# Expert blocks in two phases, the first of them ahead of the last tiles' routing, with downward products in fp16

## The chip, the cores and the metric

One core of one Trainium2 chip runs the kernel. The metric is device time in microseconds of one execution. Three runs of the kernel before gave 682.38, 676.74 and 687.29 us, median 682.38.

## What is computed

Two layers on x of 32 sequences with 128 tokens of 256 values (T = 32 tiles of 128 tokens). Each layer is an attention and a feed-forward part, each added to x. The change is in the first layer. Its feed-forward part is a mixture of E = 8 experts with hidden size H = 512, of which each token takes two:

```python
def _L0_xattn_ref(Q, K):                       # Q = layernorm(x), K = ctx
    scores = jnp.einsum('btd,bsd->bts', K, K)
    scores = scores * jnp.tril(jnp.ones((Lq, Lq)))[None, :, :]
    return Q + jnp.einsum('bts,bsd->btd', scores, Q)

def _L0_ffn_ref(x, w12, w3, gate_w):           # x = layernorm(x)
    scores = jnp.einsum('btd,ed->bte', x, gate_w)
    topk_scores, topk_idx = jax.lax.top_k(scores, TOP_K)      # TOP_K = 2
    topk_probs = jax.nn.softmax(topk_scores, axis=-1)
    ...
    h12 = jnp.einsum('btd,ehd->bteh', x, w12)
    h1, h2 = (h12[..., :H], h12[..., H:])
    hidden = jax.nn.silu(h1) * h2
    expert_out = jnp.einsum('bteh,edh->bted', hidden, w3)
    return jnp.sum(total_probs[..., None] * expert_out, axis=-2)
```

## The kernel before

There is one instruction stream for each engine; engines wait for each other by semaphores written out by hand, so the order in the code is the order on the engine.

**The attention** (`sync0`, `pool0`, `act0`, `pe0`, `dve0`) goes over 32 tiles in steps s. TensorE makes the scores (L588), the gate products (L598) and the product with y (L609, writes x1 together with VectorE's L666). VectorE masks scores (L662) and takes moments. In the same steps a tile's normed row z is made and split into a high and a low fp16 part (`make_z`, `high_z` on ScalarE, `low_z` L774 on VectorE), and six groups of tiles (`ROUTES`) are routed: `choose` picks the two experts of each token, TensorE's `rank` counts, `put_down` gives each row its place in its expert's region. POOL then scatters each tile's rows twice (L504, once for each choice) into `z_rows` in DRAM, which is sorted by expert. ScalarE takes the squares of w12 (L530) for its scale. The tables `z_step`, `w12_step`, `w3_step` and `square_at` say at which step each load or part stands. SyncE (SP) loads context, x and weights in its queue.

**Between** attention and blocks the last tiles are routed and scattered. For the first PRE = 3 experts ScalarE and VectorE split w12 in high and low fp16 parts (L538, L782) and w3 in two fp32r parts (L540, L785). `block_tables` finds for each of NB = 71 blocks of 128 rows its first row, its expert and its scale.

**The expert blocks** (`sync1`, `pool1`, `act1`, `pe1`, `dve1`), j = 0 to 70, sorted by expert. SP's `load(j)` turns 128 rows of z by DMA (four buffers), `load_told` fetches each row's token number and gap, eight blocks at a time. VectorE's `hold` (L1176) copies the block's expert w12 into one of two buffers. TensorE's `up` is 48 products of 128 columns (L1084), ScalarE takes the silu (L1136), VectorE the hidden row (L1184, `hidden`), ScalarE its high part (L1143), VectorE its low part (L1190, `rest_g`), and TensorE's `down` is 12 products of 256 columns (L1097). `keep_y` (L1152) weighs the result. TensorE's order is up(j + 1), down(j). Before a block eight `weigh` operations (L1197 on) turn told rows into weights. POOL splits the weights of experts 3 to 7 (`prepare`, L1038 to L1043), and then hands the blocks' rows out to their tokens by an adding DMA (`hand_out`, L1053). A block of expert e waits in `hold` until `w_ready` counts e + 1.

**The second layer** follows (222 us) and is the same in both kernels.

## Time and profile of the kernel before

The profiled execution took 683.7 us; the median of the runs is 682.4.

| engine | busy us | share of the span | instructions |
|---|---|---|---|
| TensorE (PE) | 559.4 | 82% | 5902 |
| weight loads (PEld) | 487.4 | 71% | 5902 |
| VectorE (DVE) | 509.4 | 75% | 1475 |
| ScalarE (ACT) | 359.4 | 53% | 662 |
| GpSimd (POOL) | 391.1 | 57% | 469 |

The DMA engines moved 87.2 MB. In 40 slices of 17.1 us each, in tenths of busy time, TensorE stands at

```profile
PE   5887772055989999999999999990777676899997
DVE  5997867666698877666666565642999688999997
POOL 1064554779999998888884434332002023888655
PEclk9765665568999999999999999996799999999999
```

The first row has a hole at slices 7 and 8 (120 to 137 us) and one at 27 (462 to 479). PEclk is the granted TensorE clock in tenths of full speed. An average over the span mixes stretches with different limits, so the rows below are taken by stretch.

### The profile page before, as it was taken

To read this page: it belongs to the slowest core of one execution; us is meant where nothing else is said; L and a number is where in the kernel's file an instruction comes from. 1 tells how busy PE (TensorE), PEld (TensorE's weight loads), DVE (VectorE), ACT (ScalarE), POOL (GpSimd) and SP (SyncE) were. 2 spreads that over 40 slices of the span, in tenths; PEclk is the share of its full clock that TensorE was granted. 3 is DMA by queue.
4 is the path that set the end of the run, shared out by engine and by line. 5 is a ranking of instruction groups with operands and counts; after the bars stand their busy time and mean duration, and the time that the engine had idled before them with its cause. 6 is when DMAs were issued, how large, how long until landed. Compare 5 with 4: busy or idle time off the path is not lost.

```text
span 683.7 us, 17743 instructions
## 1 busy us (share of the span) xinstructions
PE 559.4 (82%) x5902; PEld 487.4 (71%) x5902; DVE 509.4 (75%) x1475; ACT 359.4 (53%) x662; POOL 391.1 (57%) x469
## 2 busy tenths in 40 slices
PE   5887772055989999999999999990777676899997
PEld 5776661035989999999999999990655453566765
DVE  5997867666698877666666565642999688999997
ACT  2254647622334444434444444430667957999995
POOL 1064554779999998888884434332002023888655
PEclk9765665568999999999999999996799999999999
DMA  8598993436444514787986654447795300011112
GB/s 308 185 310 295 360 363 132 149 78 156 86 127 88 133 26 61 91 101 90 104 98 78 67 64 65 72 86 199 232 356 168 102 17 1 10 47 40 40 39 79
DMA packets 103166, 87.23 MB, mean 128 GB/s; under 512 B 55075, under 2 KB 94883, under 8 KB 102054
## 3 DMA queue, kind: packets, MB, share of 16 engines
q1 hardware_dynamic: 89782, 68.27, 35.7%
q0 software_dynamic: 13296, 17.83, 16.2%
q8 instruction: 50, 0.82, 0.5%
q14 instruction: 38, 0.31, 0.2%
HBM read 44.35 MB, written 32.41 MB: 112 GB/s over the span
## 4 chain that ended last, share of the span: by engine, by line
PE 58%; DVE 19%; issue 8%; ACT 5%; DMA 2%; SPq 2%; DVEq 0%; ACTq 0%; another core or an unknown queue 0%; POOLq 0%
PE banks L1084 25%; PE banks L1097 14%; PE banks L1726 4%; PE banks L1702 3%; PE banks L1705 2%; PE banks L1716 2%; PE banks L598 1%; ACT work L555 1%; PE banks L609 1%; DVE w_parts L782 1%; DVE h_rounded L1990 1%; DVE ffn_amax L1963 1%; ACT hidden_ffn L1595 1%; DVE x_rows L1754 1%; DVE hidden_T_low L1190 1%
## 5 line engine op out<-in xcount | busy, mean ns | idle before, releaser
L1084 PE MATMUL banks<-z_turned,w_of_block 128*128 128x128 f16 x3408 | 203.9, 220 | 0.7 <-DMA z_turned<-z_rows 0.3
L1084 PEld LDWEIGHTS banks<-z_turned,w_of_block 128*128 128x128 f16 x3408 | 192.0, 98 | 4.4 <-issue 1.5
L1053 POOL DMA_INDIRECT rows_of_tokens<-x_rows,row_tokens x71 | 121.4, 1710 | 77.9 <-ACT x_rows L1152 50.6
L1184 DVE SCALAR_TENSOR_TENSOR hidden_T<-banks,blk_inv,silu_T 128x512 f32<-128x512 f32 x71 | 53.3, 751 | 87.7 <-PE banks L1084 87.3
L1143 ACT ACTIVATE hidden_T_high<-hidden_T 128x512 fp32r<-128x512 f32 x71 | 44.9, 632 | 124.5 <-DVE hidden_T L1184 114.7
L504 POOL DMA_INDIRECT z_rows<-z_parts,places_in_regions x64 | 66.1, 1033 | 76.2 <-DVE z_parts L774 44.0
L1176 DVE COPY w_of_block<-w_parts 128x4096 f16 x71 | 97.8, 1379 | 6.6 <-issue 3.7
L1097 PE MATMUL banks<-w_low,hidden_T_high 128*128 x284 | 86.4, 304 | 10.6 <-DVE hidden_T_low L1190 10.5
L1136 ACT ACTIVATE silu_T<-banks,blk_inv 128x512 f32<-128x512 f32 x71 | 48.8, 687 | 64.9 <-PE banks L1084 54.7
L1097 PE MATMUL banks<-w_high,hidden_T_high 128*128 x284 | 79.8, 281 | 0.0
L1097 PE MATMUL banks<-w_high,hidden_T_low 128*128 x284 | 79.6, 280 | 0.0
L1097 PEld LDWEIGHTS banks<-w_low,hidden_T_high 128*128 128x128 f32 x284 | 54.1, 190 | 12.1 <-issue 11.8
L1190 DVE TENSOR_TENSOR hidden_T_low<-hidden_T,hidden_T_high 128x512 fp32r<-128x512 f32 x71 | 60.3, 849 | 1.7 <-ACT hidden_T_high L1143 1.7
L1097 PEld LDWEIGHTS banks<-w_high,hidden_T_high 128*128 128x128 f32 x284 | 54.2, 191 | 0.0
L1097 PEld LDWEIGHTS banks<-w_high,hidden_T_low 128*128 128x128 f32 x284 | 53.9, 190 | 0.0
L1456 POOL TENSOR_TENSOR x_centred<-x_rows,ffn_mean 128x256 f32<-128x256 f32 x32 | 20.2, 639 | 49.8 <-DVE ffn_tmp L1904 47.8
L609 PE MATMUL banks<-work 128*128 128x264 f32 x64 | 34.1, 631 | 12.1 <-DVE work L680 7.3
L555 ACT ACTIVATE work<-x_rows,norm_biases,norm_scales 128x256 f32<-128x256 f32 x32 | 18.9, 591 | 43.9 <-DVE norm_biases L750 22.6
L1464 POOL TENSOR_SCALAR x_rounded<-x_centred,ffn_k 128x256 f32<-128x256 f32 x32 | 16.2, 506 | 44.3 <-DVE ffn_k L1943 38.3
L1595 ACT ACTIVATE hidden_ffn<-banks,ffn_alpha 128x1024 f32<-128x1024 f32 x32 | 35.2, 1101 | 7.5 <-PE banks L1705 6.5
L1963 DVE TENSOR_REDUCE ffn_amax<-hidden_ffn 128x1 f32<-128x1024 f32 x32 | 38.7, 1210 | 0.1
L1702 PE MATMUL banks<-w_ternary,x_steps_T 128*128 128x512 f16 x128 | 33.8, 387 | 6.0 <-ACT hidden_ffn L1595 4.7
(270 smaller groups left out, 1226.2 us busy)
## 6 DMA issues: line engine op xcount, KB each, us to landing
w_parts<-in_w SPq DMA_DIRECT2D x7, 1024.0 KB, 9.1
x_rows<-in_x SPq DMA_DIRECT2D x8, 512.0 KB, 5.2
w_parts<-in_ctx_and_x_turned SPq DMA_DIRECT2D x8, 512.0 KB
w_high<-in_ctx_and_x_turned SPq DMA_DIRECT2D x8, 512.0 KB
w_low<-in_w SPq DMA_DIRECT2D x8, 512.0 KB
rows_of_tokens<-x_rows SPq DMA_DIRECT2D x8, 512.0 KB, 4.0
rows_of_tokens<-zero_rows SPq DMA_DIRECT2D x8, 512.0 KB, 3.7
w_last_in<-in_ctx_rows SPq DMA_DIRECT2D x32, 128.0 KB, 3.8
```

What stands on the lines that cost most here:

```text
L504: pool.indirect_dma_start(z_rows[:, :], bass.IndirectOffsetOnAxis(ap=put_at[:, t, k:k + 1], axis=0), zp[:, t % ZP, :], None).then_inc(scat ...
L1053: pool.indirect_dma_start(token_rows[:, :], bass.IndirectOffsetOnAxis(ap=dest[:, j:j + 1], axis=0), X1[:, j % T, :], None, compute_op=ALU. ...
L1084: mm = pe.matmul(PS[:, 1 + half + 2 * u, hc * P:(hc + 1) * P], win[:, u, wp, c, at:at + P], zturn[:, j % ZB, k, :], start=(n == 0), stop=( ...
L1097: mm = pe.matmul(PS[:, 6 + u, 0:D], gg[:, u, c * P:(c + 1) * P], w[:, e, c, :].rearrange("p a d -> p (a d)"), start=(n == 0), stop=(n == 3 ...
L1136: a.activation(s[:, :], PS[:, 1 + 2 * u, :], ACT.Silu, scale=blk_inv[:, j:j + 1])\
L1143: a.activation(gh[:, u, :], g[:, :], ACT.Copy).then_inc(gh_made, 1)
L1176: v.tensor_copy(win[:, u, :, :, :].rearrange("p a c h -> p (a c h)"), W12[:, bass.ds(e[j % READ], 1), :, :, :].rearrange("p b a c h -> p ( ...
L1184: v.scalar_tensor_tensor(out=g[:, :], in0=PS[:, 2 + 2 * u, :], scalar=blk_inv[:, j:j + 1], in1=s[:, :], op0=ALU.mult, op1=ALU.mult).then_i ...
L1190: v.tensor_tensor(gl[:, u, :], g[:, :], gh[:, u, :].bitcast(F32), ALU.subtract).then_inc(gl_made, 1)
L1595: a.activation(h[:, t % R, :], PS[:, 1:3, :].rearrange("p a b -> p (a b)"), ACT.Gelu, scale=al[:, t % R:t % R + 1]).then_inc(gelu_made, 1)
L1702: pe.matmul(PS[:, 1 + half, :], x1T[:, t % 2, c * P:(c + 1) * P], w1q[:, c, half * 512:(half + 1) * 512], start=(c == 0), stop=False)
L1963: v.tensor_reduce(am2[:, t % R:t % R + 1], h[:, t % R, :], AX_X, ALU.max, apply_absolute_value=True)\
```

## The change

- The blocks run in two phases. Phase one has NB1 = 32 blocks: only full blocks, of the rows of the first SOON = 20 tiles, in the order of experts (`taken` counts them for each expert). Phase two has the other 39 blocks with all rows left. By the reference's inputs phase one takes 5, 3, 6, 4, 4, 4, 4 and 2 blocks of experts 0 to 7.
- Tiles 20 to 31 get their z parts, and tiles 26 to 31 their routing, beside the blocks of phase one (`late_z`, `more`). POOL scatters these 12 tiles after its preparations. SP waits before the load of block 32 until all of it has landed.
- Loads, squares, scales and the splitting of experts 0 to 2 move into the attention's steps.
- w3 is scaled and split into two fp16 parts as w12 is, the hidden rows into two fp16 parts. `weigh` has eight operations instead of seven.
- The 16 warming products are gone (`WARM`). The context buffers lie in `w12_of_block`.

```diff
 PRE = 3
-WEIGH = 7
-WARM = 16
+SOON = 20
+NB1 = 32
+WEIGH = 8
...
-        W3H = sbm("w3_high", [P, E, HC, D], F32R)
-        W3L = sbm("w3_low", [P, E, HC, D], F32R)
+        W3 = sbm("w3_parts", [P, E, 2, HC, D], F16)
...
+        gh = sb("hidden_T_high", [P, 2, H], F16)
+        gl = sb("hidden_T_low", [P, 2, H], F16)
...
-        w12_step = {8: 0, 10: 1, 12: 2, 15: 3, 18: 4, 21: 5, 23: 6, 25: 7}
-        w3_step = {14: 0, 17: 1, 20: 2, 27: 3, 28: 4, 29: 5, 30: 6, 31: 7}
...
+        w12_step = {0: 0, 3: 1, 5: 2, 8: 3, 10: 4, 12: 5, 14: 6, 16: 7}
+        w3_step = {2: 0, 4: 1, 7: 2, 9: 3, 11: 4, 13: 5, 15: 6, 17: 7}
...
+        total_step = {14: 0, 27: 1}
+        high_step = {16: (0, 0), 18: (0, 1), 20: (1, 0), 21: (1, 1), 24: (2, 0), 25: (2, 1)}
+        low_step = {18: (0, 0), 19: (0, 1), 20: (0, 2), 22: (1, 0), 23: (1, 1), 24: (1, 2), 26: (2, 0), 27: (2, 1), 28: (2, 2)}
+        TABLE_STEP = 29
...
+                if j == NB1:
+
+                    sp.wait_ge(tables, TABLE2)
+                    sp.wait_ge(tails, TAILS)
+                if j % READ == 0:
+                    rows.extend(block_values(mybir.EngineType.SP, blk_row, j, Z_ROWS - P))
+                load(j)
...
+                for kind, raw, high, low, parts in ((0, raw12(e), part12(e, 0), part12(e, 1), 4),
+                                                    (1, raw3(e), part3(e, 0), part3(e, 1), 2)):
+                    for n in range(parts):
+                        cols = slice(n * H, (n + 1) * H)
+                        ch.link(pool.tensor_tensor(raw[:, cols], raw[:, cols], wsc[:, kind, e:e + 1].broadcast_to([P, H]), ALU.mult))
+                        ch.link(pool.tensor_copy(high[:, cols], raw[:, cols]))
+                        ch.link(pool.tensor_tensor(low[:, cols], raw[:, cols], high[:, cols], ALU.subtract))
...
+            for t in range(SOON):
+                scatter(t)
+
+
+            pool.wait_ge(w_high, 2 * PRE)
+            pool.wait_ge(w_low, 3 * PRE)
+            pool.wait_ge(scaled, SCALE * len(GROUPS))
+            for e in range(PRE, E):
+                prepare(e)
+            for t in range(SOON, T):
+                scatter(t)
+
+
+            for k in range(ZP):
+                pool.wait_ge(scattered[k], MOVED[k])
+            pool.sem_inc(tails, 16)
+            for g0 in range(NQ):
+                pool.wait_ge(rows_in[g0], 32)
+            pool.wait_ge(zeroed, 16 * NQ)
+            for j in range(NB):
+                hand_out(j)
...
+                if j in late_z:
+                    make_z(late_z[j])
+                    high_z(late_z[j])
...
+                if j + 1 < NB:
+                    hidden(j + 1, 1 - u)
+                    if j < SPREAD_AT:
+                        more(j)
+                if j + 3 < NB:
+                    hold(j + 3, 1 - u)
+                    if j < SPREAD_AT:
+                        more(j)
+                if j + 1 < NB:
+                    rest_g(j + 1, 1 - u)
+                    if j < SPREAD_AT:
+                        more(j)
+                if j - 1 in late_z:
+                    low_z(late_z[j - 1])
+                if (j + 2) % READ == 0 and j + 2 < NB:
+                    weigh((j + 2) // READ)
```

GpSimd's queue from the scatters on, before (x64 is all 32 tiles, twice each; then the preparation of expert 3, of which the first and the last part are shown):

```order
L504 DMA z_rows<-z_parts,places_in_regions 34688x260 x64
L1038 TENSOR_TENSOR w_parts<-w_parts,w_scale 128x512
L1039 CAST w_parts<-w_parts 128x512
L1040 TENSOR_TENSOR w_parts<-w_parts 128x512
...
L1042 CAST w_high<-w_low 128x256
L1043 TENSOR_TENSOR w_low<-w_low,w_high 128x256
...
L1053 DMA rows_of_tokens<-x_rows,row_tokens 17280x256 x71
```

And after (the last rows of expert 7's preparation, then the late scatters):

```order
L583 DMA z_rows<-z_parts,places_in_regions 34688x260 x40
L594 TENSOR_TENSOR w_parts<-w_parts,w_scale 128x512
L595 CAST w_parts<-w_parts 128x512
L596 TENSOR_TENSOR w_parts<-w_parts 128x512
...
L594 TENSOR_TENSOR w_last_in<-w_last_in,w_scale 128x512
L595 CAST w_parts<-w_last_in 128x512
L596 TENSOR_TENSOR w_parts<-w_last_in,w_parts 128x512
L583 DMA z_rows<-z_parts,places_in_regions 34688x260 x24
L605 DMA rows_of_tokens<-x_rows,row_tokens 17280x256 x71
```

24 of the 64 scatters now stand behind all five preparations.

VectorE at an early block, before:

```order
L1184 SCALAR_TENSOR_TENSOR hidden_T<-banks,blk_inv,silu_T 128x512
L1174 REGISTER_ALU x2
L1176 ISA
L1176 COPY w_of_block<-w_parts 128x4096
L1190 TENSOR_TENSOR hidden_T_low<-hidden_T,hidden_T_high 128x512
```

And after, with links of the last batch's norms and of the last route's choice among them:

```order
L1226 SCALAR_TENSOR_TENSOR hidden_T<-banks,blk_scales,silu_T 128x512
L953 TENSOR_SCALAR rstds<-vars 128x6
L1069 TENSOR_REDUCE told<-route_work 128x6
L1216 REGISTER_ALU x2
L1218 ISA
L1218 COPY w_of_block<-w_parts 128x4096
L956 TENSOR_SCALAR rstds<-rstds 128x6
L1072 TENSOR_TENSOR first<-rev_expert,told 128x48
L1232 TENSOR_TENSOR hidden_T_low<-hidden_T,hidden_T_high 128x512
L959 TENSOR_TENSOR tmps<-rstds 128x6
L1078 SCALAR_TENSOR_TENSOR route_work<-first,logits 128x48
```

Small operations now stand between the three large ones of a block.

VectorE in an attention step after (step 22), where a low part of expert 1's w12 stands among the step's work and the norms' links; before, no such part stands in the attention:

```order
L899 TENSOR_TENSOR x_rows<-banks,x_rows 128x256
L950 SCALAR_TENSOR_TENSOR vars<-mean_gaps,vars 128x12
L917 TENSOR_TENSOR logits<-banks,x_by_gate 128x8
L1030 TENSOR_TENSOR z_parts<-work,z_parts 128x256
L953 TENSOR_SCALAR rstds<-vars 128x12
L929 BN_STATS moments_in<-x_rows 128x6
L956 TENSOR_SCALAR rstds<-rstds 128x12
L1038 SCALAR_TENSOR_TENSOR w_parts<-w_parts,w_scale 128x1024
L959 TENSOR_TENSOR tmps<-rstds 128x12
```

Nine such parts stand in steps 18 to 28.

## Rows read from the trace of the kernel before

**Rows 1.** Windows: us, busy (x) of PE, PEld, DVE, ACT, POOL, clock, DMA share, GB/s

```profile
0.00:110.00 110.00, 81.97 (x387) 69.72 (x387) 84.56 (x453) 54.11 (x111) 42.61 (x62) 0.71 0.80 286
...
110.00:147.90 37.90, 5.88 (x21) 2.66 (x22) 24.91 (x91) 21.34 (x33) 26.53 (x25) 0.50 0.41 142
150.60:461.70 311.10, 300.01 (x4260) 295.13 (x4260) 210.66 (x275) 122.41 (x212) 226.92 (x168) 0.99 0.59 88
461.70:683.70 222.00, 169.15 (x1228) 119.12 (x1228) 186.92 (x656) 161.53 (x307) 92.50 (x215) 0.95 0.32 102
```

**Rows 2.** Timeline of VectorE, the last x1 row: start us, us, what

```profile
109.01 0.42 DVE L666 TENSOR_TENSOR x_rows<-banks,x_rows 128x256 f32<-128x256 f32 x1 [0.89 <-PE banks L609]
```

**Rows 3.** Chain of waits around the blocks' start, in steady blocks, at the end

```profile
144.12 3.43 DMA z_rows<-z_parts,places_in_regions
...
167.46 2.92 PE banks L1097 x12
170.39 4.18 PE banks L1084 x48
...
254.74 2.70 PE banks L1084 x48
257.43 1.46 PE banks L1097 x12
...
460.00 1.68 PE banks L1097 x12
```

**Rows 4.** Groups by line: busy us, mean ns | idle before, releaser

```profile
L1053 POOL DMA_INDIRECT rows_of_tokens<-x_rows,row_tokens x71 | 121.4, 1710 | 77.9 <-ACT x_rows L1152 50.6 <-issue 17.9 <-DVE hits L1197 4.9
L1176 DVE COPY w_of_block<-w_parts 128x4096 f16 x71 | 97.8, 1379 | 6.6 <-issue 3.7 <-DMA z_rows<-z_parts,places_in_regions 3.0
L1190 DVE TENSOR_TENSOR hidden_T_low<-hidden_T,hidden_T_high 128x512 fp32r<-128x512 f32 x71 | 60.3, 849 | 1.7 <-ACT hidden_T_high L1143 1.7
L1184 DVE SCALAR_TENSOR_TENSOR hidden_T<-banks,blk_inv,silu_T 128x512 f32<-128x512 f32 x71 | 53.3, 751 | 87.7 <-PE banks L1084 87.3
L1726 PE MATMUL banks<-w_ternary,h_steps_T 128*128 128x256 f16 x256 | 33.5, 274 | 0.0
L530 ACT ACTIVATE w_high<-w_parts 128x1024 bf16<-128x1024 f32 x14 | 14.6, 1040 | 0.0
L774 DVE TENSOR_TENSOR z_parts<-work,z_parts 128x256 f16<-128x256 f32 x32 | 13.2, 416 | 3.7 <-ACT z_parts L561 3.2 <-issue 0.5
L782 DVE SCALAR_TENSOR_TENSOR w_parts<-w_parts,w_scale 128x1024 f16<-128x1024 f32 x6 | 7.5, 1291 | 1.5 <-ACT w_parts L538 1.5
```

**Rows 5.** Timeline of POOL: a scatter, then parts of three preparations

```profile
121.12 0.96 POOL L504 DMA_INDIRECT z_rows<-z_parts,places_in_regions  x1 [0.30 <-DVE z_parts L774]
...
147.86 1.04 POOL L1038 TENSOR_TENSOR w_parts<-w_parts,w_scale 128x512 f32<-128x512 f32 x1 [1.78 <-DMA z_rows<-z_parts,places_in_regions]
...
159.97 1.04 POOL L1038 TENSOR_TENSOR w_parts<-w_parts,w_scale 128x512 f32<-128x512 f32 x1
...
162.97 0.40 POOL L1042 CAST w_high<-w_low 128x256 fp32r<-128x256 f32 x1
...
215.95 1.04 POOL L1038 TENSOR_TENSOR w_parts<-w_parts,w_scale 128x512 f32<-128x512 f32 x1 [0.18 <-POOL w_low L1043]
...
233.10 0.40 POOL L1042 CAST w_high<-w_low 128x256 fp32r<-128x256 f32 x1
```

**Rows 6.** Timeline of SP and VectorE, first loads and first weighing

```profile
147.85 6.40 SPq L1001 DMA_TRANSPOSE z_turned<-z_rows  x4
...
154.45 4.11 SPq L1004 DMA_DIRECT2D told_in<-z_rows  x8
...
161.99 0.95 DVE L1197 TENSOR_TENSOR hits<-told_in,blk_code 128x8 f32<-128x8 f32 x1 [4.90 <-DMA told_in<-z_rows]
...
164.12 0.15 DVE L1204 TENSOR_TENSOR row_weights<-hits,shares 128x8 f32<-128x8 f32 x1
```

**Rows 7.** Timeline of PE in the second layer, eight fp16 products

```profile
622.58 1.05 PE L1726 MATMUL banks<-w_ternary,h_steps_T 128*128 128x256 f16 x8
```

More of the change, by code:

```diff
@@ new lines, in pick @@
+                    yield
+                dve.wait_ge(lg_made, t1)
+                yield from pick(LG[:, tt, :], m1, c1, first)
+                ch.join()
+                ch.post(v.scalar_tensor_tensor(out=a2[:, 0:n, :], in0=first[:, tt, :], scalar=-HUGE,
+                                               in1=LG[:, tt, :], op0=ALU.mult, op1=ALU.add))
+                yield
+                yield from pick(a2[:, 0:n, :], m2, c2, second)
+                ch.join()
+                ch.post(v.tensor_tensor(both[:, tt, :], first[:, tt, :], second[:, tt, :], ALU.add))
@@ new lines, in put_told, with tell_tails @@
+            def put_told(r):
+                dve.wait_ge(exped, r + 1)
+                for p0, p1 in pieces[r]:
+                    slots = slice(p0 % ZP, p0 % ZP + p1 - p0)
+                    if p1 > ZP:
+                        for t in range(p0, p1):
+                            dve.wait_ge(scattered[t % ZP], 32 * (t // ZP))
+                    v.tensor_copy(zp[:, slots, D:ZW // 2].bitcast(F32), told[:, p0:p1, :]).then_inc(told_put, 1)
+            def tell_tails():
+                dve.wait_ge(put, PUT * len(ROUTES))
+                v.tensor_copy(tail_row[:, :], next_row[:, len(ROUTES) % 2, :]).then_inc(tables, 1)
```

1541 lines of the change are left out of this document (786 added, 755 removed).

## The prediction

> **What bounds the kernel now.** I read the busy table of four stretches first [rows 1], because an average over the whole span hides that they have different limits. Stretch one (to 110 us) is the first attention; its last row of x1 is written at 109.0 us [rows 2], 3.4 us for each of 32 tiles, with VectorE busy for 84.6 of the 110 us. In stretch two (110 to 148) TensorE works 5.9 of 37.9 us: the last tiles are routed and scattered and three experts' weights are split. Stretch three is the expert blocks: 71 blocks in 311 us, TensorE busy for 300. The chain of waits says what paces them [rows 3]: a block is 2.70 us of upward and 1.46 us of downward products, back to back, 4.16 us. The fourth (222 us, the second layer) is not touched. So TensorE bounds stretch three, a serial preparation stretch two, and mostly VectorE stretch one.
>
> **The change, part by part.**
>
> *Downward products in fp16.* The 12 products of a block take 1.46 us, 122 ns each, in fp32r [rows 3]. The nearest fp16 row with 256 columns is eight products in 1.05 us, the end of the last one included [rows 7]; one of them has 274 ns [rows 4], so the pitch is (1.05 - 0.27) / 7 = 110 ns, and 12 take 1.33 us. That is 0.13 us a block; the bounds are 0 (the same pitch as now) and 0.2 (a pitch of 105 ns, below any row's). I take 4.03 us a block. The number of products is the same.
>
> *Work moved into the attention.* On VectorE nine low parts of the first three experts now stand in steps 18 to 28, at 1.29 us each, 11.6 us [rows 4]; two chains of 13 scale operations and a table of 22 add 48 small operations at 0.2 us, 9.6 us (between the 0.15 that one is busy and the 0.33 of one in a bare chain, seven in 2.3 us [rows 6]); three low z parts fewer take 1.2 off [rows 4]. Together +20 us on an engine that is busy for 84.6 of 110 [rows 1]. Its 25 idle us are mostly the start and waits for TensorE; I let them take in 3.5, so x1 ends at 109.4 + 16.5 = 126 us. Bounds: +4 (nearly all the idle time outside the start takes it in) and +25. ScalarE gets eight more squares of 1.04 us [rows 4] and six roundings, some 18 us, but is busy for 54 of 110 [rows 1] and makes y up to four tiles ahead: nothing, or up to 5 us if that lead is gone. The DMA queues move 7 of the 12 MB of weights from the attention's later half to its earlier half; their share is 0.80 over the stretch [rows 1], so the reserve is there, and I take nothing, at most 5 us.
>
> *First blocks.* In the kernel before the blocks begin at 150.6 [rows 1], after the last scatter's landing at 147.6 [rows 3]. Now only the tables (step 31) and the scatters of tile 19 (step 29) are needed, both ready by the attention's end; a weight copy of 1.38 us [rows 4] and a register load stand between. First product at about 129.5. Its told rows wait in SP's queue behind four transposes as before [rows 6], but the transposes now leave before the attention ends.
>
> *POOL, the part that decides.* Its queue is now: scatters of 20 tiles, five preparations, 24 scatters, then the hand-outs. SP's load of block 32 waits for those 24 scatters, and behind it on SP stand its told rows and every later block. (a) Preparations start when tile 19 is scattered, some 8 us (three steps) before x1's end: 118. (b) Each is now six parts of three operations (four of w12, two of w3, 512 columns). One part took (162.97 - 147.86) / 4 = 3.78 us when VectorE was half idle, and (233.10 - 215.95) / 4 = 4.29 in the steady blocks [rows 5]. Three parts before the attention's end at 3.4, 27 at 4.25: 125 us, to 243. (c) 24 scatters: 16 pitches from 121.12 to 144.12 are 1.44 us each [rows 3, 5], with VectorE splitting weights beside them; with a weight copy in every block I take 1.5, 36 us, to 279. Bounds 1.26 (0.96 and an issue gap of 0.30 [rows 5]) and 2.0 (the hand-outs: 1.71 [rows 4] and the same gap). (d) Landing of the last 3.4 [rows 3]: 282.
>
> The preparation's speed depends on VectorE: the shortest part is 3.00 us (159.97 to 162.97), a part beside steady blocks 4.29 [rows 5]. The Trainium skill (SBUF — State Buffer, Who interferes with whom) says that a VectorE copy in a two-port mode and a GpSimd operation exclude each other for their whole length. By that rule POOL would lose the copy's 1.38 of every 4.16 us, so a part would be 3.00 / (1 - 0.33) = 4.5 instead of 4.25, an estimate by which the result would be 7 us later; the trace agrees in kind and shows a little less.
>
> *Does the wait show?* Phase one: block 0 at 129.5. VectorE's own block is 1.38 + 0.75 + 0.85 = 2.98 us [rows 4]; in blocks 2 to 13 a low z part (0.42) and three route links (0.25 each, between the same 0.15 and 0.33) come to it, with gaps 4.5, above TensorE's 4.03. So 12 blocks at 4.5, 7 at 4.25, 13 at 4.05, plus 6 for the start and 6 for three weighings: 148 us, to 278. The preparations are ahead of the blocks: by the reference's inputs experts 3 and 7 are first wanted at blocks 14 and 30, copied near 185 and 252, ready near 143 and 243. TensorE then wants block 32 and gets it at 282 + about 4: a wait of some 9 us.
>
> *Phase two.* After the landing at 282 come, in order: a register load and one transpose (2.3), eight told loads (4.1), their landing (3.4) and the weighing (2.3) [rows 6], then hidden, copy, rest (3.0) [rows 4]: the downward products of block 32 start 15.1 us later. From there 39 downward (1.33) and 37 upward (2.70) groups: 151.8. The last block's own wait is 2.5 (0.75 and 0.85 [rows 4] with ScalarE's rounding and the hops between them); a cold clock at the restart costs up to 2.9 (2.92 + 4.18 against 1.46 + 2.70 [rows 3], with the granted clock low in stretch two [rows 1]), I take 2. End: 282.4 + 15.1 + 151.8 + 2.5 + 2 = 453.8. Hand-outs start near 284, at 2.0 us each: they catch up with blocks of 4.03 near block 57, so they delay nothing at the end. In the kernel before they ended at 460.00 + 1.68 = 461.7 [rows 3].
>
> **Sum.** The attention's end is 16.5 us later, its blocks start 21 earlier, the boundary gives most of that back: 453.8 + 222.0 [rows 1] = 675.8 us against 683.7 of the profiled execution, which stands 1.3 above the median 682.4. I say 675.
>
> **The rivals.**
> - *The attention absorbs the work* (+4 instead of +16.5) and scatters run at 1.3 us: 12.5 + 5 earlier, 658. For it: 25 idle us on VectorE, and low parts set in steps without routing. Against: in 20 to 110 us every added operation stands in the same queue as the score mask that TensorE waits for.
> - *POOL and VectorE block each other harder* (slower): the preparations run beside a VectorE busy 4.5 us a block, not 3. If a part takes 5.2 us, 27 parts add 26 us: 701. It turns slower than 2% from a part of about 5.0. Against: from half idle to steady VectorE a part grew only by 0.5 [rows 5].
> - *A much longer attention* (+30: ScalarE's roundings and the earlier weights hold up y and c): 689.
> - *The boundary never waits* and TensorE paces all 71 blocks from 129.5: 129.5 + 6 + 71 x 4.03 + 2.5 = 424, plus 8 for the blocks that VectorE paces, plus 222: 654. It needs POOL done by about 255.
>
> **Chances.** The likeliest 0.46 (own range 667 to 687), absorbed attention 0.26, harder blocking 0.13, longer attention 0.10, no wait 0.05. Two per cent is about what a measurement of this kernel tells from no change: below 669 lie the second and fifth cases and a little of the first, 0.34; above 696 the harder blocking, 0.13; between, 0.53. The range that leaves out 2 in 10: 656 to 694.
>
> **What would show it.** In the profile after: x1's last row near 126; POOL's first preparation near 118 and its last scatter near 279; a gap on TensorE before block 32 of about 10 us, released by a z load; downward groups of 1.33 us; last downward product near 454. A part longer than 5 us, or x1's end beyond 140 or before 115, would make the time wrong; so would TensorE waiting for an expert in phase one.

## The result, and the profile after

The changed kernel takes 696.5 us (median of four runs, 695.5 to 698.3) against 680.8 for the kernel before: a ratio of 1.0225 with a 95% interval of 1.016 to 1.029. It is slower: the interval lies wholly above 1 and takes in 2%, about what a measurement of this kernel can tell. The time lies outside the range of 656 to 694 that was forecast. The profiled execution has a span of 694.6 us, which answers to the 683.7 of before.

The windows of the changed kernel, cut where its stages end (columns as in [rows 1]):

```profile
0.00:119.99 119.99, 90.83 (x393) 75.92 (x393) 99.98 (x507) 72.14 (x134) 53.28 (x68) 0.68 0.71 263
119.99:142.60 22.61, 11.32 (x156) 10.77 (x156) 15.56 (x28) 3.48 (x6) 21.17 (x19) 0.80 0.68 164
142.60:238.90 96.30, 79.97 (x1062) 71.65 (x1063) 88.08 (x132) 41.21 (x78) 89.06 (x71) 0.92 0.33 87
238.90:267.70 28.80, 10.25 (x68) 5.53 (x68) 4.32 (x6) 2.42 (x4) 20.37 (x20) 0.64 0.33 105
267.70:472.00 204.30, 201.62 (x2986) 193.29 (x2986) 129.23 (x200) 84.74 (x152) 116.60 (x70) 0.99 0.66 87
472.00:694.60 222.60, 170.56 (x1228) 119.81 (x1228) 186.73 (x656) 161.29 (x307) 92.56 (x215) 0.93 0.32 102
```

Read them against [rows 1]. The second layer is the same, 222.6 against 222.0 us. The attention is some 10.6 us longer. The last stretch of the blocks is as dense as a stretch can be (201.6 of 204.3 us). In the third row VectorE is the engine that is full: 88.1 of 96.3 us, TensorE 80.0. The fourth row is what nobody had forecast: in 28.8 us TensorE makes 68 products, 54 upward, 12 downward and two small ones, which are 4.3 us of work at the pace of steady groups, while VectorE and ScalarE are nearly idle, POOL is busy, and the DMA engines are a third busy.

POOL in the changed kernel, the first operation of the preparations, then their last and the first late scatter:

```profile
113.72 1.05 POOL L594 TENSOR_TENSOR w_parts<-w_parts,w_scale 128x512 f32<-128x512 f32 x1
...
229.97 1.55 POOL L596 TENSOR_TENSOR w_parts<-w_last_in,w_parts 128x512 f16<-128x512 f32 x1
232.44 1.89 POOL L583 DMA_INDIRECT z_rows<-z_parts,places_in_regions  x1 [0.91 <-POOL w_parts L596]
```

Thirty parts in 117.8 us, 3.93 each; then 24 scatters, until 265.06. The timeline of all engines inside the fourth row:

```profile
257.80 0.96 POOL L583 DMA_INDIRECT z_rows<-z_parts,places_in_regions  x1 [0.30 <-issue]
257.81 0.10 PEld L812 LDWEIGHTS banks<-z_turned,w_of_block 128*128 128x128 f16 x1 [2.94 <-issue]
258.52 0.26 PE L812 MATMUL banks<-z_turned,w_of_block 128*128 128x128 f16 x1 [1.82 <-issue]
259.06 0.96 POOL L583 DMA_INDIRECT z_rows<-z_parts,places_in_regions  x1 [0.30 <-issue]
259.18 0.01 SPq L476 DMA_DIRECT2D told_in<-z_rows  x1
259.22 0.10 PEld L812 LDWEIGHTS banks<-z_turned,w_of_block 128*128 128x128 f16 x1 [1.30 <-issue]
259.92 0.26 PE L812 MATMUL banks<-z_turned,w_of_block 128*128 128x128 f16 x1 [1.14 <-issue]
```

These are products in the middle of one group (line 812): their weights and inputs are in place, no wait stands between them, and what ended each idle time is "issue". Steady upward products come some 56 ns apart. Here a weight load and its product stand 0.70 us apart, and the next pair 1.4 us behind. This is the stall at its deepest; at its start, from 239 to 246 us, TensorE still makes some forty products between its pauses. SP, too, issues slowly: eight told loads take 12.15 us in one row from 256.38, against 4.11 in [rows 6]. POOL meanwhile issues a scatter every 1.26 us. In this run TensorE is at full speed again when the last one has landed; the chain of waits, before, inside and after:

```profile
233.50 2.68 PE banks L812 x48
236.18 1.31 PE banks L825 x12
...
256.69 1.82 issue
...
267.66 2.52 PE banks L812 x22
270.18 1.68 PE banks L825 x12
271.86 2.68 PE banks L812 x48
```

A steady block is 2.68 + 1.31 = 3.99 us, as against 2.70 + 1.46 in [rows 3].

### The profile page after: what moved, and what is told of

Same layout as the page of the kernel before. It is cut to its first block, busy times and chain, and to the rows that moved or that the text cites. A ratio compares the mean times of both kernels' runs of the same rounds, so it can differ in the third digit from the quotient of the medians.

```text
span 694.6 us, 17785 instructions
## 1 busy us (share of the span) xinstructions
PE 564.6 (81%) x5890; PEld 477.0 (69%) x5890; DVE 523.9 (75%) x1524; ACT 365.3 (53%) x680; POOL 393.0 (57%) x459
## 4 chain that ended last, share of the span: by engine, by line
PE 50%; DVE 19%; issue 9%; ACT 4%; SPq 2%; DMA 2%; DVEq 1%; ACTq 0%; POOLq 0%
PE banks L812 22%; PE banks L825 11%; PE banks L1858 4%; PE banks L1834 3%; DVE hidden_T_low L1232 2%; PE banks L1837 2%; PE banks L1848 1%; PE banks L1774 1%; DVE hidden_T L1226 1%; DVE ffn_amax L2095 1%; DVE w_of_block L1218 1%; ACT hidden_ffn L1727 1%; PE banks L1767 1%; DVE h_rounded L2122 1%; DMA expert_rows_in<-rows_of_tokens 1%
## 5 line engine op out<-in xcount | busy, mean ns | idle before, releaser
L1226 DVE SCALAR_TENSOR_TENSOR hidden_T<-banks,blk_scales,silu_T 128x512 f32<-128x512 f32 x71 | 53.2, 749 | 105.4 <-PE banks L812 85.4
L688 ACT ACTIVATE hidden_T_high<-hidden_T 128x512 f16<-128x512 f32 x71 | 44.8, 630 | 157.3 <-DVE hidden_T L1226 134.3
L825 PE MATMUL banks<-w_parts,hidden_T_high 128*128 x568 | 101.7, 280 | 26.0 <-DVE hidden_T_low L1232 24.7
L825 PEld LDWEIGHTS banks<-w_parts,hidden_T_high 128*128 128x128 f16 x568 | 54.4, 100 | 37.2 <-issue 29.5
L825 PE MATMUL banks<-w_parts,hidden_T_low 128*128 x284 | 79.3, 279 | 0.3 <-issue 0.3
L681 ACT ACTIVATE silu_T<-banks,blk_scales 128x512 f32<-128x512 f32 x71 | 48.6, 684 | 52.4 <-PE banks L812 39.7
L1232 DVE TENSOR_TENSOR hidden_T_low<-hidden_T,hidden_T_high 128x512 f16<-128x512 f32 x71 | 55.9, 787 | 1.8 <-ACT hidden_T_high L688 1.7
L697 ACT ACTIVATE x_rows<-banks,row_weights 128x256 f32<-128x256 f32 x71 | 32.6, 459 | 17.6 <-remote 12.9
L744 PEld LDWEIGHTS banks<-w_of_block 128*128 128x128 f32 x128 | 31.7, 314 | 6.8 <-issue 2.2
L744 PE MATMUL banks<-w_of_block 128*128 128x128 f32 x128 | 33.2, 410 | 2.2 <-DMA w_of_block<-in_ctx_and_x_turned 2.2
```

Of the source, the lines that this page charges most:

```text
L681: a.activation(s[:, :], PS[:, 1 + 2 * u, :], ACT.Silu, scale=blk_scale[:, 0, j:j + 1])\
L688: a.activation(gh[:, u, :], g[:, :], ACT.Copy).then_inc(gh_made, 1)
L744: pe.matmul(bank, chunk, chunk, start=(c == 0), stop=False)
L825: mm = pe.matmul(PS[:, 6 + u, 0:D], gg[:, u, c * P:(c + 1) * P], W3[:, e, wp, c, :].rearrange("p a d -> p (a d)"), start=(n == 0), stop=(n ...
L1226: v.scalar_tensor_tensor(out=g[:, :], in0=PS[:, 2 + 2 * u, :], scalar=blk_scale[:, 1, j:j + 1], in1=s[:, :], op0=ALU.mult, op1=ALU.mult).t ...
L1232: v.tensor_tensor(gl[:, u, :], g[:, :], gh[:, u, :], ALU.subtract).then_inc(gl_made, 1)
```

## The experiments

Two things are to be explained: the stall (theory B: POOL's back-to-back scatters cause it; theory C: something else in that stretch does), and the long phase one (theory A: VectorE's operations wait out POOL's). Each ratio is to the kernel before, run beside it.

### A gap for the stall, twice the scatters, and the scatters alone

```
 e1:      for t in range(SOON, T):
+             pool.wait_ge(ye_made, 18 + t - SOON)
              scatter(t)
 e2:      for t in range(SOON, T):
              scatter(t)
+         (the same 24 scatters again, to spare_rows, and a wait for their landing)
 e3 (kernel before):
          pool.wait_ge(zeroed, 16 * NQ)
+         pool.wait_ge(weighed, WEIGH * 3)
+         pool.wait_ge(ye_made, 24)
+         for j in range(24):
+             pool.indirect_dma_start(spare_rows[:, :], IndirectOffsetOnAxis(ap=dest[:, j:j + 1], axis=0), X1[:, j % T, :], None)
+         (and a wait for their landing)
          for j in range(NB): hand_out(j)
```

> The changed kernel, with one edit: of the 24 late scatters, the pair of tile t waits until block t-3's row is kept (tile 20 behind block 17, one pair for each later block). Theory B (POOL's late scatters, back to back at 1.26 us from 232 to 265 us, hold up the issue of TensorE's products, and a gap between them lets the products through): the stretch from 239 to 268 us, in which TensorE did some 4.5 us of work, shrinks to a few us, so 696.5 - 24 = 672 us, and up to 680 where block 32 then waits for the last pair. Theory B2 (each scatter costs TensorE its 1 us wherever it stands): 694 to 698 us, the idle time only spread out. Theory C (the stall has nothing to do with the scatters: instruction loads, the clock, the second table's products at 246.5 us): 694 to 700 us, with the stall at block 20 to 22 as before.

> The changed kernel with 24 more scatters of the same late rows into a spare tensor, behind the 24 late ones (work that nothing reads; the outputs are the same). Theory B and B2: TensorE stays held up for as long again, 24 x 1.26 = 30 us: about 725 us, with TensorE idle until some 298 us. Theory C: 696 to 700 us, TensorE at full speed from 268 us, since the hand-outs behind them have 28 us to catch up in.

> The kernel before with 24 more scatters (rows of 1024 bytes, plain writes into a spare tensor that nothing reads) issued back to back by POOL between its preparations and its hand-outs, from some 264 us, among steady blocks. Theory B: TensorE's products fall to a few per scatter there as in the changed kernel, and the time rises by 25 to 30 us to about 708 us: the effect belongs to the scatters, not to the change's other parts. Theory C: 680 to 690 us, TensorE at full speed beside the scatters, at most a wait of block 32's row for the hand-outs that start some 33 us later.

Measured: e1 677.8 us (ten runs; ratio 0.991, 0.987 to 0.995), e2 738.7 (1.080, 1.070 to 1.089), e3 713.8 (1.044, 1.034 to 1.053). The windows of e1 over its scatters, of e2 and of e3:

```profile
234.50:285.00 50.50, 48.68 (x711) 45.25 (x709) 30.86 (x48) 19.70 (x35) 26.14 (x24) 1.00 0.41 108
```

```profile
245.00:300.00 55.00, 9.96 (x48) 4.49 (x48) 2.48 (x3) 1.79 (x3) 40.10 (x42) 0.54 0.31 102
```

```profile
271.00:298.00 27.00, 8.33 (x52) 5.24 (x52) 2.65 (x3) 1.32 (x2) 20.33 (x21) 0.61 0.30 104
```

Theory B holds, and C falls: with the pairs a block apart TensorE is busy for 48.7 of 50.5 us beside the same 24 scatters; with 48 in a row it is held for more than 55 us; and in the kernel before, which has nothing else of the change, 24 indirect writes among steady blocks leave 52 products in 27 us. B2 (each scatter costs its 1 us anywhere) falls with e1. By the ratios, 0.991 against 1.0225, the gap gives back 21 us. What e1 has left is a wait at block 32, as expected: the last pair is issued at 284.37, and the first transposes and told loads of phase two follow on SP, so TensorE is busy for 10.2 of the 15 us after 285.

e2 took some 14 us more than the 725 expected, because its stall outlasts the writes. The last one is issued at 295.18 us, and from 298.86 on the hand-outs follow, some 1.9 us apart; TensorE is free only at 314:

```profile
268.00:298.00 30.00, 3.19 (x12) 1.19 (x12) 0.00 (x0) 0.47 (x1) 21.44 (x23) 0.50 0.29 102
298.00:314.00 16.00, 4.93 (x21) 2.54 (x22) 0.00 (x0) 0.69 (x1) 12.70 (x9) 0.50 0.52 57
```

In the changed kernel and in e1 TensorE is at full speed beside hand-outs at that same pitch. So a stall, once it is there, can go on beside writes that don't set one off. The same two rows bear on one rival, missing instruction loads, which theory C names. The DMA view of e2 from 245 to 314 us lists no load on the two instruction queues, and TensorE goes on all the while (from 268 to 298 at one product per 2.5 us), so the instructions it executed there had been loaded before.

### The fp16 products alone

```
-  for gg, w in ((gh, W3L), (gh, W3H), (gl, W3H)):     (fp32r)
+  for gg, wp in ((gh, 1), (gh, 0), (gl, 0)):          (W3, gh and gl in fp16)
```

> The kernel before with one part of the change alone: the downward products' operands as fp16 high and low parts (weights and hidden rows, without the change's scaling by powers of two), no second phase. The down group goes from 1.46 to 1.31 us, so a steady block from 4.16 to 4.01 us; some 50 of the 72 blocks are bounded by TensorE: 681 - 0.15 x 50 = 673 us (672 to 676) if the products set the pace there. Rival (the blocks are set by VectorE or by waits): 679 to 682 us.

Measured: 676.9 us, ratio 0.989 (0.982 to 0.996). A downward group in its chain of waits, and its window over all 71 blocks:

```profile
331.05 1.31 PE banks L1096 x12
```

```profile
151.36:452.10 300.74, 289.64 (x4260) 274.39 (x4260) 211.39 (x275) 120.08 (x212) 223.49 (x168) 0.99 0.61 91
```

The blocks take 300.7 us, 10.4 fewer than the 311.1 of [rows 1]: 0.15 us for each of the 71, where the expectation had counted 50 blocks and 7.5 us. This part of the change is worth 1% by itself.

### What makes phase one long

e5 is e1 with the body of `prepare(e)` removed and `blk_exp` limited to the first three experts. It leaves out the weights of the other five, so its outputs are not those of the layer.

> The kernel of e1 without POOL's preparation of experts 3 to 7 (left out; blocks of those experts multiply by expert 2's weights, so outputs differ and the work per block is the same). Theory A (phase one is paced by VectorE because its operations wait out POOL's: the 128x512 subtraction at 1.09 instead of 0.68 us, the copy at 1.44 instead of 1.22, small two-input ones at 0.4 to 1.1 instead of some 0.15): blocks 0 to 19 go from 5.4 to 4.3 us each, block 19 ends about 20 us earlier (226 instead of 246 us), and with the late pairs following the blocks the whole takes 677.8 - 20 = 658 us. Rival (phase one is long because VectorE does the late routing, a count of operations and waits that POOL doesn't stretch): block 19 ends within 6 us of 246, and the time is 672 to 678 us.

Measured: 642.8 us (ratio 0.953, 0.945 to 0.961). The window from the first product to the last of the same 1258, in e1 and then in e5:

```profile
124.04:242.10 118.06, 94.67 (x1258) 85.58 (x1259) 102.39 (x156) 46.39 (x87) 105.63 (x86) 0.91 0.43 103
```

```profile
117.55:208.50 90.95, 86.84 (x1258) 82.46 (x1259) 64.11 (x157) 47.19 (x89) 4.34 (x4) 0.96 0.54 134
```

The same products and one VectorE instruction more, 27.1 us sooner, where 20 were expected: VectorE needs 64.1 instead of 102.4 us. (Most of the rest of the 35 us is the attention, whose last x1 row came at 113.17 in e5's profile and at 119.64 in e1's; by the ratios, 0.953 against 0.991, the difference is 26 us.) The groups by line of VectorE from 142.6 to 205 us in the changed kernel, and from 150 to 205 in e5:

```profile
L1218 DVE COPY w_of_block<-w_parts 128x4096 f16 x12 | 17.7, 1473 | 0.0
L1232 DVE TENSOR_TENSOR hidden_T_low<-hidden_T,hidden_T_high 128x512 f16<-128x512 f32 x11 | 11.6, 1051 | 0.0
L1226 DVE SCALAR_TENSOR_TENSOR hidden_T<-banks,blk_scales,silu_T 128x512 f32<-128x512 f32 x12 | 8.9, 741 | 3.9 <-ACT silu_T L681 3.1 <-PE banks L812 0.9
L1030 DVE TENSOR_TENSOR z_parts<-work,z_parts 128x256 f16<-128x256 f32 x9 | 8.1, 903 | 0.0
...
L968 DVE TENSOR_TENSOR tmps<-rstds 128x6 f32<-128x6 f32 x1 | 1.1, 1109 | 0.0
```

```profile
L1210 DVE COPY w_of_block<-w_parts 128x4096 f16 x14 | 17.1, 1218 | 0.5 <-issue 0.5
L1218 DVE SCALAR_TENSOR_TENSOR hidden_T<-banks,blk_scales,silu_T 128x512 f32<-128x512 f32 x13 | 9.8, 751 | 12.2 <-PE banks L804 8.1 <-ACT silu_T L673 3.6 <-issue 0.3
L1224 DVE TENSOR_TENSOR hidden_T_low<-hidden_T,hidden_T_high 128x512 f16<-128x512 f32 x14 | 9.6, 683 | 0.0
L1022 DVE TENSOR_TENSOR z_parts<-work,z_parts 128x256 f16<-128x256 f32 x10 | 4.2, 416 | 0.0
```

Theory A holds. The subtraction goes from 683 to 1051 ns, the low z part from 416 to 903, an operation on 128x6 elements can take 1.1 us, and `hidden_T`, whose one input is in PSUM, stays at 0.75. That agrees with what the Trainium skill says (SBUF — State Buffer, Who interferes with whom): a VectorE instruction with two inputs in SBUF contends with a GpSimd instruction that reads SBUF. The 3.1 us in which `hidden_T` waits for `silu_T` is a second, small cost that the forecast had left out: the exponential of the last route among the blocks brings two loads of activation tables on ScalarE, 1.28 us each.

### What of the writes starves TensorE

```
 e6  = e3 with rows X1[:, j % T, 0:16]            (64 bytes)
 e7  = e3 + two POOL memsets of 128x256 behind each write
 e8  = changed kernel; scatter(SOON + part) behind each of expert 7's six parts,
       then, for the last six tiles:  pool.wait_ge(ye_made, 19 + t - SOON - 6); scatter(t)
 e9  = changed kernel + three memsets of 128x128 behind each late scatter
 e10 = changed kernel + one such memset
```

> The run e3 (kernel before, 24 more indirect writes back to back among steady blocks) with rows of 64 bytes instead of 1024. If the bytes or the DMA engines' time hold TensorE up, the stall shrinks to a sixteenth and the time is 681 to 690 us. If it is the issue of indirect writes as such (128 descriptors each, made by POOL at 1.26 us a write), the stall stays some 27 us and the time is 705 to 715 us.

> The run e3 (24 more writes of 1024-byte rows) with two small POOL memsets between writes, so that they are issued at about 1.9 us, the pitch of the hand-outs beside which TensorE is at full speed, instead of 1.26 us. If TensorE is held up only by a queue that fills when writes come faster than they drain, its products run at full speed beside them and the time is 683 to 693 us (the hand-outs start some 47 us late). If every write costs TensorE its time, the stall is 27 us or more and the time 708 to 725 us.

> The changed kernel with the late scatters spread: the pairs of tiles 20 to 25 one behind each of the six parts of expert 7's preparation, those of tiles 26 to 31 one behind each kept row of blocks 18 to 23. By theory B no two pairs stand back to back, TensorE isn't starved, and the last one lands about 271 us instead of 287 in run e1, before block 32's rows are wanted, so the wait of some 5 to 7 us at that block in e1 goes too: 677.8 - 6 = 672 us (668 to 675). If pairs beside the preparations cost as much as the back-to-back ones: 676 us or more.

> The changed kernel, its 24 late scatters still in one run behind the preparations and with no wait on blocks, but with three small POOL memsets between them, so that they are issued at some 1.9 to 2.0 us (run e7's pitch, beside which TensorE ran at full speed) instead of 1.26. If only the pitch decides: no stall, the last one lands near 232 + 24 x 1.95 + 3 = 282 us, block 32 is reached no earlier than that, and the time is 696.5 - 24 = 672 us (667 to 678). If the scatters of these rows (1040 bytes) starve TensorE at that pitch too: 685 us or more.

> The same with one memset between scatters, pitch some 1.5 to 1.6 us: 128 rows of 1040 bytes each 1.55 us are 86 GB/s, between the 105 GB/s of the run at 1.26 us, which stalls, and the 68 GB/s at 1.94 us, which doesn't. If the stall sets in where the rows come faster than they drain at about 105 GB/s: no stall, 672 us as in the run with three memsets. If it grows in proportion to the rate: some half of the 24 us, 684 us.

Measured: e6 683.3 and e7 703.8 us (one run each; 676.5 for the kernel before), e8 660.5 (0.979, 0.973 to 0.986), e9 681.8 (1.008, 1.005 to 1.012), e10 666.2 (0.985, 0.971 to 0.999). In e7 TensorE is busy for all of the 42 us from 262, beside the writes. The window over the writes of e10:

```profile
227.50:272.00 44.50, 44.45 (x662) 42.31 (x660) 29.27 (x45) 18.49 (x33) 37.99 (x48) 1.00 0.65 125
```

With a gap there is no stall in any of them, and with 64-byte rows (e6) none either: TensorE is busy for all of the 36 us from 262. But VectorE's copies stretched e6's writes to a mean pitch of 1.52 us ((296.79 - 261.89) / 23), so e6 alone doesn't separate size from pitch. e7 came out above the 693 expected, and not by a stall: its writes end at 317, block 32 needs the row that hand-out 0 frees, and TensorE waits 21.4 us for it. The pitch I had counted on was also off: the memsets wait out VectorE's operations, so in e7 a write came every 2.28 us in the mean, not 1.9; in e9 a scatter came every 2.61 us in the mean (288.53 - 228.44 over 23) and the last landed after block 32 was wanted (TensorE busy 8.0 of the 22 us from 280). In e10 it is 1.89 us, and nothing waits. One small memset behind each scatter thus turns the slower kernel into a faster one.

I had then thought that e3 against e6 shows bytes to matter. The next pair of runs made me doubt how:

```
 e11 = e8 + 24 indirect writes of nil[:, :] (1040-byte rows) ahead of hand_out(20)
 e12 = e8 + the same bytes by 24 act.dma_start, three behind each of blocks 34 to 41
```

> The kernel of e8 with 24 indirect writes of 128 zero rows of 1040 bytes into a spare tensor that nothing reads, issued by POOL back to back ahead of hand-out 20 (about 315 us, in the steady blocks). The hand-outs resume some 31 us later, 20 blocks before anything waits for them. As in e3, TensorE should be starved for some 24 to 28 us: 660.5 + 26 = 686 us (682 to 692). This is the twin of e12.

> The kernel of e8 with the same 24 x 128 rows of 1040 bytes written to a spare tensor, but as plain DMAs that ScalarE issues, three behind each of blocks 34 to 41 (one per 1.35 us in the mean), while POOL's hand-outs go on. If what starves TensorE is the rate of bytes written to DRAM in such rows, it stalls as in e11: 684 us or more. If it is the indirect writes' own path (the descriptors that POOL makes, the software queue): TensorE keeps its 3.99 us a block and the time is 660 to 666 us.

Measured: e11 669.7 us (eight runs, 669.2 to 672.6), e12 661.8 (two runs). The window of e11 over its 24 writes, then of e12:

```profile
308.70:345.60 36.90, 36.90 (x562) 35.68 (x560) 24.85 (x44) 15.79 (x28) 29.58 (x24) 1.00 0.47 122
```

```profile
297.00:330.00 33.00, 33.00 (x493) 31.80 (x491) 21.75 (x34) 13.46 (x24) 28.12 (x17) 1.00 1.11 189
```

Plain DMAs from ScalarE's queue, in bursts of three per block and moving 189 GB/s with the hand-outs, disturb nothing. But e11 has no stall either, against the expectation. Its 9 us over e8 come at the end: the hand-outs, held back by the 24 writes, don't catch up, and the last is issued at 447.44 us instead of 438.98, so the second layer starts later. Three more runs asked why:

```
 e13 = e11 with X1[:, 20 + n // 2, :] as source (after a wait for block 31's row, and with a
       wait for the writes' landing ahead of hand_out(20))
 e14 = e11 with its 24 writes ahead of hand_out(0)
 e16 = e3 with nil[:, 0:D] as source
```

> Run e11 (24 indirect writes back to back ahead of hand-out 20, TensorE undisturbed) with the rows of x in twelve tiles as source, 1024 bytes each, instead of one buffer of zeros. If the source (other rows, other data) is what e11 lacked against e3: the stall of 24 to 28 us returns, 690 us or more. If it is the place in the program or the pitch (e11's writes took 1.55 us each in the mean, e3's 1.3): no stall, 663 to 673 us.

> Run e11 with its 24 writes of zero rows ahead of hand-out 0 instead of hand-out 20: no hand-out is under way before or beside them, as in e3 and in the changed kernel. If the hand-outs' traffic is what kept e11 from the stall: 690 us or more with TensorE at a few products per write. If the source's data is what matters: TensorE runs at full speed beside them, and the only loss is a wait of block 32 for the hand-outs, up to 10 us: 660 to 675 us.

> Run e3 (the kernel before, 24 writes of 1024-byte rows ahead of the hand-outs, TensorE stalled for 27 us) with one buffer of zeros as source, everything else as there. If the stall depends on the source: none here, the time falls from 714 to 683 to 692 us (the hand-outs start 33 us late as in e6). If it depends on where the writes stand: 705 to 716 us.

Measured (one run each): 716.2, 713.6 and 719.1 us. All three stall; from 318, 277 and 275 us on, in 27 us each, TensorE makes 45, 68 and 47 products. So neither the source alone nor the place alone decides. What differs is how the writes fall between VectorE's copies. Successive writes of e11, then of e14, on POOL's timeline:

```profile
326.89 1.82 POOL L635 DMA_INDIRECT spare_rows<-zero_rows,places_in_regions  x1 [0.30 <-issue]
329.02 0.96 POOL L635 DMA_INDIRECT spare_rows<-zero_rows,places_in_regions  x1 [0.31 <-issue]
330.29 1.71 POOL L635 DMA_INDIRECT spare_rows<-zero_rows,places_in_regions  x1 [0.30 <-issue]
```

```profile
277.44 0.96 POOL L635 DMA_INDIRECT spare_rows<-zero_rows,places_in_regions  x1 [0.30 <-issue]
278.70 0.96 POOL L635 DMA_INDIRECT spare_rows<-zero_rows,places_in_regions  x1 [0.30 <-issue]
```

In e11 every second or third write is stretched to 1.5 to 2.0 us; over all 24 the pitch is 1.55. In the runs that stall, nearly all are at 1.26. This suggests a loop (theory D): a few writes in a row at 1.26 us starve TensorE; VectorE, which waits for TensorE, goes idle; and only VectorE's operations ever stretch POOL's writes, so they stay at 1.26 until they are used up. The kernel of e8 fits it from the other side: in the profiles of e13 and e14, which contain it, its own last pairs came 1.26 us apart from 255 and from 251 us on, and TensorE made 42 products in each of them in the ten us from 260. No run separates cause and effect here: that VectorE is idle is also what the stall itself brings.

```
 e17 = e8 + one memset of 128x128 behind each late scatter
 e18 = e17 + 24 indirect writes of 64-byte rows ahead of hand_out(0)
 e19 = e8 again, beside e17
```

> Run e8's placing of the late scatters (a pair behind each of the six parts of expert 7, the last six pairs one per kept block from block 18 on), and a small POOL memset behind every one of them, so that no two are issued at 1.26 us. Theory D (the stall feeds itself: at 1.26 us a write TensorE starves, VectorE goes idle, and only VectorE's copies ever stretch POOL's writes to 1.5 us or more): this kernel never falls into it. 658 to 664 us, every run alike, faster than both kernels. Rival (the memsets delay the last pair past block 32's wish, as in e9): 668 or more.

> The kernel of e17 with 24 indirect writes of 64-byte rows back to back ahead of hand-out 0, the place where e14's rows of 1040 bytes stalled TensorE. If the size of the rows counts: TensorE at full speed, though several writes in a row are issued at 1.26 us; 661 to 672 us with the wait for the late hand-outs. If only the issue of descriptors counts: a stall as in e14, 690 us or more.

> Run e8's kernel once more, beside e17 on the same chip. By theory D it stands near the edge: from 250 us its last pairs are issued back to back with only VectorE's copies between them, and in the two kernels of e13 and e14, built on it and started 5 us later, TensorE stalled there for some 8 us. So 660 us in undisturbed runs and 668 to 672 in some; e17 should be as fast or faster in the median and closer together.

Measured: e17 667.2 us (six runs, 664.3 to 669.1; ratio 0.985, 0.981 to 0.989), e18 685.1 (two runs), e19 660.0 (six runs, 658.1 to 664.4; 0.976, 0.972 to 0.981). The rival of e17 was right: its last scatter came at 273.68, so block 32 waited for its rows (TensorE busy for 15.2 of the 20 us from 270). And e19 was not at the edge in its timed runs, where I had expected some at 668 to 672: none of the ten runs of e8's kernel took more than 664.4, and in its second profile (e19) TensorE makes 152 products in the ten us from 260. The stall at this place was seen only in the two kernels that contain it, one run each, and why those two fell into it stays open. e18 answers the question of size. From 277.36 to 284.93 its 64-byte writes were issued 1.26 us apart, seven in a row, and from 291.15 on again. TensorE's first group there, 48 upward products behind a wait for block 32's rows, took 4.47 us at a granted clock of 0.62, close to the 4.18 of such a group in [rows 3]; from 283.3 on it ran at full speed, beside the second run of writes too:

```profile
283.30:291.00 7.70, 7.43 (x111) 6.87 (x109) 5.59 (x8) 2.31 (x4) 6.03 (x6) 1.00 0.41 76
291.00:295.80 4.80, 4.75 (x74) 4.45 (x71) 0.00 (x0) 0.00 (x0) 3.73 (x4) 1.00 0.17 34
```

Behind 295.8 TensorE has nothing to do: ScalarE waits 22 us for the row that hand-out 0 frees. That wait, and no stall, put e18 above the 672 expected. So in the blocks of these runs a stall sets in only where long rows and a pitch of 1.26 us, several times in a row, come together. In the attention even that does nothing (see "The stall" below). Once set in, a stall can outlast them (e2; in e14 TensorE makes 15 products in the 10.8 us behind the last write). What stays open is the mechanism behind it. The DMA engines are 0.30 to 0.33 busy over the writes of a stall, and the scatters of the changed kernel land as fast as they are issued (105 GB/s, which is 128 rows of 1040 bytes each 1.26 us), so their bandwidth isn't it; TensorE waits for no semaphore; and ScalarE's and VectorE's few operations there take their usual time. Something that TensorE's and SP's issue have in common with these writes is short, and no run here shows what.

## Why the prediction was wrong, point by point

- **Attention.** 126 was forecast for x1's last row; it came at 119.57. Its end moves by itself from run to run (113.2 to 120.9 in the kernels with the changed attention, 102.8 to 110.5 in those with the old one), which may be much of the noise between runs; with one profile for most kernels that isn't shown. The added work was absorbed more than I took, less than the rival of 4 us had it.
- **First product.** 124.0 instead of 129.5. The transposes leave at 120.99, not before the attention's end, which gives back a part.
- **fp16 downward products.** 1.31 instead of 1.33 us forecast. Right, and e4 shows the gain whole.
- **POOL's preparations and scatters.** A part took 3.93, not 4.25; the late scatters' pitch 1.38 in the mean ((264.10 - 232.44) / 23), not 1.5. They were done at 265, the hand-outs began at 267.9, and no wait for block 32 showed, where 9 us and a chain of 15.1 were forecast. The rule of the Trainium skill that the prediction cites made me look at POOL's loss. The two engines also block each other the other way, and that was the way that counted: POOL's parts were faster than forecast and VectorE's operations slower.
- **Phase one.** This is the first term that failed. I costed VectorE's block with the means over all 71 blocks, 1.38 + 0.75 + 0.85 [rows 4], the low z part with its mean in an attention where POOL does little, 0.42, and small links at 0.25. Beside preparations they are 1.47, 0.74, 1.05, 0.90 and up to 1.1. The rows to take were those of the stretch in which before's POOL prepares; its trace had them, from 165 to 250 us:

```profile
L1176 DVE COPY w_of_block<-w_parts 128x4096 f16 x20 | 31.8, 1592 | 0.9 <-issue 0.9
L1190 DVE TENSOR_TENSOR hidden_T_low<-hidden_T,hidden_T_high 128x512 fp32r<-128x512 f32 x19 | 22.6, 1192 | 0.0
```

  From the first product to 238.9 us TensorE made 1218 products, 20.3 blocks' worth; by the forecast's pace (6 for the start, blocks 0 and 1 at 4.05, 2 to 13 at 4.5, then 4.25) they are 6 + 2 x 4.05 + 12 x 4.5 + 6.3 x 4.25 + 4 for two weighings = 98.9 us, and they took 114.9: 16.0 us late. e5 prices the whole contention at 27.1.
- **The stall.** This is the second, and the one that decides the sign: no term, rival or bound had it. I costed the scatters by what they do to POOL and to SP, never by what they do beside a busy TensorE; in the kernel before the last 23 of the 64 ran where TensorE works 5.9 of 37.9 us [rows 1]. The other 41 ran in the attention, up to four of them 1.26 us apart, and there TensorE wasn't held up:

```profile
85.00:92.00 7.00, 7.00 (x31) 6.24 (x31) 3.15 (x13) 6.04 (x14) 5.30 (x6) 0.54 1.01 416
```

  TensorE made 31 long products in these 7 us, where the blocks have over 100. So that trace had no row that shows the stall, and this one seemed to clear the scatters. In the changed kernel's attention six stand 1.26 us apart from 49.07 us on, and TensorE is busy for 7.12 of the 7.60 us from 49, with 28 products. That it takes the dense short products of the blocks to be held up fits these rows; no run tests it. In the changed kernel the stall holds TensorE for 28.8 us in which 4.3 us of work is done: 24.5.
- **Phase two.** From there the forecast had 453.8 - (129.5 + 98.9 + 4.3) = 221.1 us, with the boundary's wait of 9 us and its chain of 15.1; it took 204.3: 16.8 less. Neither came: at 267.7 TensorE had made 1286 products, 21.4 blocks' worth, some ten blocks short of the one that needs the late rows. In e10, which has no stall, neither came either (TensorE busy for 44.45 of 44.50 us up to 272).

The sum by stages: -5.5 (first product) + 16.0 + 24.5 - 16.8 + 0.6 (second layer) = 18.8, which is 694.6 against 675.8. Without the stall the errors of the other steps nearly cancel, at 670, and e10, which removes it by one memset, has 661.8 in its profile (its attention ended at 114.5) and 666.2 in the median. The forecast's likeliest case was thus near for that kernel, by two errors of opposite sign, and wrong for the one that was asked about. The rival "harder blocking" gave 701, close to the result, but by another mechanism: it needed parts longer than 5.0 us and they were 3.9. None of the signs that I had named as ones that would make the time wrong came up. Of those that should have shown the forecast right, the last scatter (264.1 us, not 279), the gap before block 32 (none) and the last downward product (472, not 454) were missed.

**A version that beats both.** e8 keeps the two phases and the fp16 products and sends the late scatters one pair per part of expert 7 and, by its waits, one pair per kept block: 660.5 and, run again, 660.0 us, 2.1 and 2.4% faster than the kernel before, and by the ratios (0.976 over 1.0225) 4.5% faster than the changed one. In its profile the waits of the last pairs were already met: the last fourteen writes come 1.61 us apart in the mean, stretched by VectorE's copies alone, so its margin against the stall isn't known (e13 and e14). Its windows are those of a kernel bounded by TensorE from 243 us on; the first is still phase one's price:

```profile
120.67:243.40 122.73, 102.03 (x1395) 92.58 (x1396) 107.08 (x167) 50.74 (x95) 113.41 (x93) 0.93 0.43 109
243.40:265.30 21.90, 21.90 (x337) 21.20 (x334) 14.97 (x25) 9.10 (x16) 17.94 (x14) 1.00 0.69 157
265.30:437.70 172.40, 170.64 (x2544) 163.58 (x2541) 110.32 (x167) 71.76 (x128) 117.54 (x71) 1.00 0.76 92
```

## What to carry to other kernels

When a change moves work beside an engine that was idle before, cost it for what it does to that engine too, and take durations from the stretch in which the same neighbours are active, not from a mean over the span. Don't let GpSimd issue indirect writes of long rows one after another beside a TensorE that makes short products back to back: a pair per block gave back 21 us here (e1), one small GpSimd operation behind each some 25 (e10: a ratio of 0.985 instead of 1.0225). Keep the gap small where something waits for the last write: with three operations behind each (e9) TensorE waited 13.8 us for block 32's rows, and in e17 4.4. An idle time "issue" in the middle of a group of products, with no wait named, is the sign to look for what the other queues do in that window.

## What the hardware showed that was not expected

- Back-to-back indirect writes of 128 rows of 1024 or 1040 bytes, one each 1.26 us, hold TensorE to 68 products in 28.8 us in the changed kernel, at the deepest one weight load or product per 0.70 us there and one product per 2.5 us in e2, and SP's issue to a third of its speed, at a DMA share of 0.3. In e2 it goes on beside the hand-outs, from 298.86 to 314 us. The Trainium skill says (SBUF — State Buffer, Who interferes with whom) that DMA never contends with a compute engine, and that PE and ACT never wait on anyone. What the Trainium skill says there is about ports of SBUF; the trace doesn't show at what TensorE is held up, but that writes of GpSimd's queue do hold it up: 52 products in 27 us (e3) decide against the first sentence as it stands.
- In the stalls the granted clock falls, to 0.50 in e2's row from 268 to 298 us, in which TensorE makes 12 products; that is the lower of its two levels (1.2 of 2.4 GHz). The first downward group after a stall takes longer (1.68 us from 270.18 to 271.86 in the changed kernel against 1.31).
- VectorE's weight copies stretch a scatter from 0.96 to as much as 2.0 us: in the changed kernel the one of 238.49 us ends at 240.25, just behind the copy from 238.91 to 240.13. The Trainium skill (SBUF — State Buffer, SBUF: two separate sides) names it: GpSimd can't write descriptors while VectorE runs an operation in a two-port mode. The trace agrees. That this delay protects TensorE is argued, not shown: e11, whose writes it stretches to a pitch of 1.55, has no stall.
- Rows of 64 bytes at the same 1.26 us, and 3.2 MB by plain DMAs of ScalarE's queue, don't slow TensorE's groups (e18 from 283.3 us on, e12).
